# Attention scores of a transformer layer: whole float32 operands on four row groups of 32, in place of split parts over 128 rows

## The reference

```
q = (x @ Wq) -> 16 heads of 2*32;   k = (x @ Wk) -> 4 heads of 2*32;   v = (x @ Wv) -> 4 heads of 64
q1, q2 = rope(q[..., :32]), rope(q[..., 32:]);   k1, k2 likewise       # 4 heads of q share one of k and v
s1 = q1 @ k1.T / sqrt(32) + causal mask;   s2 = q2 @ k2.T / sqrt(32) + causal mask
out = (softmax(s1) - lam * softmax(s2)) @ v
out = group norm of out over time and channels, per head;   x = layernorm(x + out @ Wo)
x = layernorm(x + (silu(x @ up.T) * (x @ gate.T)) @ down.T)            # ternary up, gate, down
```

## Time and profile before

| what | us |
|---|---|
| median of 3 runs (lowest, highest) | 2625.27 (2624.8, 2626.22) |
| the profiled execution: its time, its span | 2625.6, 2623.8 |
| TensorE busy in the span | 2405.9 |
| VectorE busy | 1788.7 |
| ScalarE busy | 1412.5 |
| GpSimd busy | 814.8 |
| first and last start of a score matmul | 89.4, 2257.9 |

### The profile page before, as it was taken

How to read it: one execution, slowest core, us unless ns; L and a number is a source line. 1 busy time by engine, 2 the same in 40 slices (tenths; PEclk the granted TensorE clock), 3 DMA queues, 4 the chain that set the end, 5 groups by cost and what they waited for, 6 DMA issues and landing times.

```text
span 2623.8 us, 40656 instructions
## 1 busy us (share of the span) xinstructions
PE 2405.9 (92%) x14610; PEld 1424.2 (54%) x14610; DVE 1788.7 (68%) x3370; ACT 1412.5 (54%) x3462; POOL 814.8 (31%) x1344
## 2 busy tenths in 40 slices
PE   7689978789999999999999999999999989998999
PEld 4356554455655555555555556555555555543443
DVE  1467777878777777777777877787787777633343
ACT  1268755566655666666556666666656666420221
POOL 2323356644321333323221342323231222231122
PEclk9799988899999999999999999999999999999999
DMA  5756655555541212122622252313144311003000
GB/s 161 206 163 176 183 159 152 145 150 167 151 111 41 67 59 73 48 81 78 195 75 65 91 139 71 91 61 93 41 121 119 86 39 41 17 33 120 9 17 16
DMA packets 257591, 256.49 MB, mean 98 GB/s; under 512 B 31344, under 2 KB 199408, under 8 KB 255216
## 3 DMA queue, kind: packets, MB, share of 16 engines
q1 hardware_dynamic: 244864, 218.16, 29.5%
q10 hardware_dynamic: 12528, 35.73, 4.5%
HBM read 182.53 MB, written 71.30 MB: 97 GB/s over the span
## 4 chain that ended last, share of the span: by engine, by line
PE 70%; DVE 11%; ACT 6%; POOL 5%; issue 5%; DMA 1%; SPq 0%; ACTq 0%; POOLq 0%; DVEq 0%
PE F L703 17%; PE F L690 9%; PE PV L650 8%; PE F L712 8%; PE S L632 8%; PE F L673 7%; PE TB L617 7%; DVE nmax L953 4%; PE F L681 2%; ACT dt_long L757 2%; ACT e_short L766 2%; PE PV L653 2%; PE S L635 2%; POOL x_lo L937 2%; POOL hl L919 1%
## 5 line engine op out<-in xcount | busy, mean ns | idle before, releaser
L953 DVE TENSOR_REDUCE nmax<-S 128x1 f32<-128x1024 f32 (+7 forms) x1024 | 769.5, 752 | 434.1 <-PE S L635 429.7
L766 ACT ACTIVATE e_long<-S,nmax 128x768 f32<-128x768 f32 (+3 forms) x512 | 489.8, 957 | 301.4 <-DVE nmax L953 295.1
L632 PE MATMUL S<-kstk,qstk 128*128 128x384 f32 (+5 forms) x1536 | 552.3, 414 | 91.7 <-ACT e_long L766 71.2
L892 POOL TENSOR_SCALAR coef<-lsum,linv,neglam 128x1 f32<-128x1 f32 x512 | 176.0, 344 | 1223.0 <-DVE linv L1031 1222.3
L757 ACT ACTIVATE dt_long<-TB 128x512 f32<-128x512 f32 (+3 forms) x512 | 265.2, 518 | 425.1 <-PE TB L617 423.8
L632 PEld LDWEIGHTS S<-kstk,qstk 128*128 128x128 f32 x1536 | 268.2, 200 | 185.8 <-ACT e_long L766 65.3
L673 PE MATMUL F<-xT,wr 128*128 128x512 f32 x640 | 324.1, 637 | 4.4 <-DVE t L987 4.4
L1063 DVE SCALAR_TENSOR_TENSOR e_long<-e_long,coef 128x1024 f32<-128x1024 f32 (+3 forms) x256 | 287.6, 1123 | 37.6 <-POOL coef L892 37.4
L617 PE MATMUL TB<-ident,e_long 128*128 128x128 f32 x1664 | 272.9, 278 | 9.8 <-ACT dt_long L757 9.5
L766 ACT ACTIVATE e_short<-S,nmax 128x384 f32<-128x384 f32 (+3 forms) x512 | 269.2, 526 | 17.5 <-DVE nmax L953 17.1
L690 PE MATMUL F<-wo_sb,at_sb 128*128 128x512 f32 x512 | 243.0, 606 | 14.6 <-issue 11.0
(11 more groups left out here) (101 smaller groups left out, 3288.1 us busy)
## 6 DMA issues: line engine op xcount, KB each, us to landing
qstk<-dq SPq DMA_DIRECT2D x512, 128.0 KB, 3.2
dq<-hl SPq DMA_DIRECT2D x32, 1024.0 KB, 5.0
wr<-in_w_proj ACTq DMA_DIRECT2D x48, 512.0 KB, 3.7
kstk<-dk SPq DMA_DIRECT2D x64, 256.0 KB, 5.4
da<-ra SPq DMA_DIRECT2D x32, 512.0 KB, 2.7
at_sb<-da SPq DMA_DIRECT2D x32, 512.0 KB, 4.2
xs<-in_x ACTq DMA_DIRECT2D x36, 256.0 KB, 3.3
dk<-hl SPq DMA_DIRECT2D x8, 1024.0 KB, 4.9
```

The costliest lines, as they stand in the source:

```text
L632: nc.tensor.matmul(slot[:, h, :], qstk[:, duo % 4, 2 * r + m, :].bitcast(F32R), kstk[:, g % 2, m, h * w:(h + 1) * w].bitcast(F32R), start= ...
L766: nc.scalar.activation(e.rearrange("p (h w) -> p h w", h=parts), slot, ACT.Exp, bias=nmax[:, u % 8:u % 8 + 1], scale=1.0, accum_out=lsum[: ...
L953: nc.vector.tensor_reduce(nmax[:, u % 8:u % 8 + 1], bank_of(n, m), AX.XY, ALU.max, negate=True)\
```

## The change

q and k are no longer split. GpSimd writes the rotated values into `qk`, two DMAs store them, and the loads place the 32 rows of map 0 and the 32 rows of map 1 twice over the 128 partitions (rows 64h+32m). A head's scores are then float32 matmuls of 32 rows: row group 64h+32m computes map m of column half h into bank `S[m][:, h]`. A head with t = 0 has one half (two matmuls), any other two halves (four matmuls). Both maps of head n+1 are issued together at the end of step n, behind one wait: `s_exp >= 2n+2`, which is both exponents of head n. The matmuls in the middle of the step go. The two mask matmuls follow, and one semaphore increment tells of both maps.

The bit mask, the subtraction and the stage of the pipeline between them go, and with them one step of delay of the store. The planner's costs follow: only `score_cost(n + 1)` is charged to step n. The queues of ScalarE and, but for the bit mask, of VectorE keep their order.

```diff
 def score_cost(n):
     t = STEPS[n].t
-    return 0.0533 * (t + 1) + 0.1 * (1 + (t >= 4)) + 0.067
+    return 0.107 * (t + 1) / (2 if t else 1) + 0.35
...
-    c = 0.0
-    for k in (n, n + 1):
-        if 0 <= k < NH:
-            c += score_cost(k)
+    c = score_cost(n + 1) if 0 <= n + 1 < NH else 0.0
...
         def bank_of(n, m):
             t = STEPS[n].t
             w = (t + 1) * P
-            if t >= 4:
-                return S[m][:, :, 0:w // 2]
-            return S[m][:, n // 2 % 2:n // 2 % 2 + 1, 0:w]
+            return S[m][:, 0:halves(n), 0:w // halves(n)]
...
-                sp.wait_ge(s_lo, u + 1)
-                sp.dma_start(dst[:, :, :, job.h * BANK:(job.h + 1) * BANK].rearrange("a (e i) m t -> (i m) (a e) t", e=2),
-                             hl[:, :, :]).then_inc(s_hlst, 16)
+                sp.wait_ge(s_rot, u + 1)
+                for m in range(2):
+                    sp.dma_start(dst[m, :, :, job.h * BANK:(job.h + 1) * BANK].rearrange("(e i) h t -> (i h) e t", e=2),
+                                 qk[64 * m:64 * m + 64, u % 2, :, :]).then_inc(s_qkst[u % 2], 16)
...
-                for k in ended(st - 3, ("O",)):
+                for k in ended(st - 2, ("O",)):
                     store_rotated(k)
...
-            def scores(n, m):
-                b, c, t, r, duo = STEPS[n]
+            def scores(n):
+                t, r, duo = STEPS[n].t, STEPS[n].r, STEPS[n].duo
...
-                if SCORE_AFTER[2 * n + m]:
-                    pe.wait_ge(s_exp, SCORE_AFTER[2 * n + m])
-                slot = bank_of(n, m)
-                parts, w = slot.shape[1], slot.shape[2]
+                if n:
+                    pe.wait_ge(s_exp, 2 * n)
+                parts = halves(n)
+                w = (t + 1) * P // parts
                 for h in range(parts):
-                    nc.tensor.matmul(slot[:, h, :], qstk[:, duo % 4, 2 * r + m, :].bitcast(F32R),
-                                     kstk[:, g % 2, m, h * w:(h + 1) * w].bitcast(F32R),
-                                     start=True, stop=h < parts - 1)
-                nc.tensor.matmul(slot[:, parts - 1, w - P:w], ident_b[:, :], mask_b[:, :], start=False, stop=True)\
-                    .then_inc(s_score, 1)
+                    for m in range(2):
+                        rows = slice(64 * h + 32 * m, 64 * h + 32 * m + 32)
+                        nc.tensor.matmul(S[m][:, h, 0:w], qstk[rows, duo % 4, r, :], kstk[rows, g % 2, h * w:(h + 1) * w],
+                                         start=True, stop=h < parts - 1)
+                for m in range(2):
+                    last = nc.tensor.matmul(S[m][:, parts - 1, w - P:w], ident_b[:, :], mask_b[:, :], start=False, stop=True)
+                last.then_inc(s_score, 1)
...
-                if 0 <= n < NH:
-                    scores(n, 1)
...
                 if 0 <= n + 1 < NH:
-                    scores(n + 1, 0)
+                    scores(n + 1)
...
-                for k in ended(st - 2, ("O",)):
-                    u = ROT[k]
-                    dve.wait_ge(s_rot, u + 1)
-                    if u:
-                        dve.wait_ge(s_hlst, 16 * u)
-                    nc.vector.tensor_scalar(hl[:, 0:2, :].bitcast(I32), t4[:, 0:2, :].bitcast(I32), HI_BITS, None,
-                                            ALU.bitwise_and).then_inc(s_hi, 1)
```

More of the change, by code:

```diff
@@ L7 @@
 from concourse import mybir
-F32, F32R, F16, BF16 = mybir.dt.float32, mybir.dt.float32r, mybir.dt.float16, mybir.dt.bfloat16
-F8, I32 = mybir.dt.float8e4, mybir.dt.int32
+F32, F16, BF16 = mybir.dt.float32, mybir.dt.float16, mybir.dt.bfloat16
+F8 = mybir.dt.float8e4
 ACT = mybir.ActivationFunctionType
@@ L28 @@
 NEG = -3.0e38
-HI_BITS = -4096
 XS = 1024.0
@@ L65, with halves @@
         TURN[_n, _h] = len(TURN)
[L68 to L78, removed]
+def halves(n):
+    return 2 if STEPS[n].t else 1
 JOB = namedtuple("JOB", "kind b h i j")
@@ L287, in layer_kernel @@
              w_down.rearrange("(c p) n -> p c n", p=P)]
-    dq = nc.dram_tensor("dq", (B, 4, 2, DH, 8, T), F32, kind="Internal").ap()
-    dk = nc.dram_tensor("dk", (B, 2, DH, 8, T), F32, kind="Internal").ap()
+    dq = nc.dram_tensor("dq", (B, 4, 2, DH, 4, T), F32, kind="Internal").ap()
+    dk = nc.dram_tensor("dk", (B, 2, DH, KV, T), F32, kind="Internal").ap()
     dv = nc.dram_tensor("dv", (B, NT, P, 256), F32, kind="Internal").ap()
@@ L321, in layer_kernel @@
         t4 = sb("t4", [P, 4, BANK])
-        hl = sb("hl", [P, 4, BANK])
+        qk = sb("qk", [P, 2, 2, BANK])
         vst = sb("vst", [P, 2, 256])
-        qstk = sb("qstk", [P, 4, 4, P])
-        kstk = sb("kstk", [P, 2, 2, T])
+        qstk = sb("qstk", [P, 4, 2, P])
+        kstk = sb("kstk", [P, 2, T])
         vkv = sb("vkv", [P, 2, NT, 64])
@@ L389, in layer_kernel @@
         s_gn = sem("s_gn")
-        s_hlst = sem("s_hlst")
+        s_qkst = [sem(f"s_qkst{k}") for k in range(2)]
         s_vst = sem("s_vst")
@@ L412, in layer_kernel @@
         s_rot = sem("s_rot")
-        s_hi = sem("s_hi")
-        s_lo = sem("s_lo")
         s_xhi = sem("s_xhi")
@@ L446, in freed, with stored @@
             eng.wait_ge(s_ffree[k % 2], k // 2 + 1)
+        def stored(eng, u):
+            eng.wait_ge(s_qkst[u % 2], 32 * (u // 2 + 1))
         def bank_of(n, m):
@@ L492, in load_q @@
                 b, c, t, _, _ = STEPS[n]
-                sp.wait_ge(s_hlst, 16 * (ROT_OF[b, t // 4, 2 + c // 2] + 1))
+                stored(sp, ROT_OF[b, t // 4, 2 + c // 2])
                 if duo >= 4:
-                    sp.wait_ge(s_score, 2 * heads_of(duo - 4)[1] + 2)
-                at = 4 * (c % 2)
-                src = dq[b, c // 2, :, :, at:at + 4, t * P:(t + 1) * P].rearrange("a d m t -> (a d) m t")
+                    sp.wait_ge(s_score, heads_of(duo - 4)[1] + 1)
+                at = 2 * (c % 2)
+                src = dq[b, c // 2, :, :, at:at + 2, t * P:(t + 1) * P].rearrange("m d h t -> (m d) h t")
                 for half in range(2):
@@ L502, in load_k @@
                 b, kv = divmod(g, KV)
-                sp.wait_ge(s_hlst, 16 * (ROT_OF[b, 1, 0] + 1))
+                stored(sp, ROT_OF[b, 1, 0])
                 if g >= 2:
[L505 to L508, removed]
+                    sp.wait_ge(s_score, 32 * (g - 1))
+                src = dk[b, :, :, kv, :].rearrange("m d t -> (m d) t")
+                for half in range(2):
+                    sp.dma_start(kstk[64 * half:64 * half + 64, g % 2, :], src).then_inc(s_kin[g % 2], 16)
             def load_v(g):
@@ L618, in turn @@
                 last.then_inc(s_tb, 1)
-            def scores(n, m):
-                b, c, t, r, duo = STEPS[n]
+            def scores(n):
+                t, r, duo = STEPS[n].t, STEPS[n].r, STEPS[n].duo
                 g = n // 32
-                if r == 0 and m == 0:
+                if r == 0:
                     pe.wait_ge(s_qin[duo % 4], 32 * (duo // 4 + 1))
-                if n % 32 == 0 and m == 0:
-                    pe.wait_ge(s_kin[g % 2], 64 * (g // 2 + 1))
-                if SCORE_AFTER[2 * n + m]:
-                    pe.wait_ge(s_exp, SCORE_AFTER[2 * n + m])
-                slot = bank_of(n, m)
-                parts, w = slot.shape[1], slot.shape[2]
-                for h in range(parts):
-                    nc.tensor.matmul(slot[:, h, :], qstk[:, duo % 4, 2 * r + m, :].bitcast(F32R),
-                                     kstk[:, g % 2, m, h * w:(h + 1) * w].bitcast(F32R),
-                                     start=True, stop=h < parts - 1)
-                nc.tensor.matmul(slot[:, parts - 1, w - P:w], ident_b[:, :], mask_b[:, :], start=False, stop=True)\
-                    .then_inc(s_score, 1)
+                if n % 32 == 0:
+                    pe.wait_ge(s_kin[g % 2], 32 * (g // 2 + 1))
+                if n:
+                    pe.wait_ge(s_exp, 2 * n)
+                parts = halves(n)
+                w = (t + 1) * P // parts
+                for h in range(parts):
+                    for m in range(2):
[5 more added lines that the diff above has]
+                last.then_inc(s_score, 1)
             def values(duo):
@@ L913, in _ @@
                 for k in ended(st - 1, ("O",)):
+                    u = ROT[k]
                     freed(pool, k)
-                    nc.gpsimd.tensor_tensor(t4[:, 0, :], t4[:, 0, :], t4[:, 2, :], ALU.subtract)
-                    nc.gpsimd.tensor_tensor(t4[:, 1, :], t4[:, 1, :], t4[:, 3, :], ALU.add).then_inc(s_rot, 1)
-                for k in ended(st - 2, ("O",)):
-                    pool.wait_ge(s_hi, ROT[k] + 1)
-                    nc.gpsimd.tensor_tensor(hl[:, 2:4, :], t4[:, 0:2, :], hl[:, 0:2, :], ALU.subtract).then_inc(s_lo, 1)
+                    if u >= 2:
+                        stored(pool, u - 2)
+                    nc.gpsimd.tensor_tensor(qk[:, u % 2, 0, :], t4[:, 0, :], t4[:, 2, :], ALU.subtract)
+                    nc.gpsimd.tensor_tensor(qk[:, u % 2, 1, :], t4[:, 1, :], t4[:, 3, :], ALU.add).then_inc(s_rot, 1)
```

(9 more changed lines are left out.)

## The result

The changed kernel took 3189.03 us (median of four runs, 3188.04 to 3192.9) against 2625.74 us for the kernel before on the same chip: a ratio of 1.2148 (95% interval 1.2127 to 1.2169), so 563 us slower. The forecast was 3040 us with a range of 2860 to 3200. The profiled execution has a span of 3187.0 us.

The account below looks back on a forecast made before the run. TensorE was taken as the bound. Work 2018, new waits 610 and lower clock 50 gave 2678 us of attention; with start 89 and tail 275, 3042, stated as 3040 us, range 2860 to 3200.

Parts of the forecast that it names:

- The score work costs the same: TensorE's score matmuls: four row groups together give back what four slots a column take; 437 us against 438 before.
- The rival of one pass: Score packs cost one pass in place of two, as the planner's price says: 126 us less, 2915 us; chance 0.12.
- that of groups in pairs: Row groups of the score packs run only in pairs, or passes in turn: 253 us more, 3290 or more; chance 0.1.
- that of a poorer overlap: The four row groups overlap less well than two column groups did: about 75 us more, 3115 us; chance 0.15.
- The wait in odd steps: At the end of steps with a short head, scores wait for ScalarE's second exponent, behind an eviction: 320 us.
- The wait in even steps: At the end of steps with a long head, scores wait for VectorE's chain and the second exponent: 290 us.
- The new waits don't shrink because others run ahead: Denies the rival that ScalarE and VectorE run ahead, so new waits are half as long: 2840 us; chance 0.13.
- the 0.37 at which that case began: Faster case, 2500 us, chance 0.04: decides where the new wait is under 0.37 us a step; forecast had 1.2.
- the remainder: What the attention stretch loses beyond TensorE's work and new waits, taken as lower clock: 50 us, ends 0 and 241.
- the old 241 us: Waits, gaps and lower clock in the 2172 us in which scores ran in the kernel before.
- 2018 (work at full clock): TensorE's work in the attention stretch: fill 961, scores 437, turns 277, values 343 us.
- The plan: New planner prices move fill from tail to attention, +88 and -88 us: still TensorE's work, so no gain.

Follow-up runs that it names:

- e9: e1 with one wait more: VectorE's maximum of map 0 waits for the scores of both maps; 3188 us.
- e7: The changed kernel with the planner's old prices, so fill stands where it stood before; 3206 us.
- e3: The changed kernel with ScalarE's exponent of map 1 put ahead of the eviction of the second half of head n-3; 2942 us.
- e4: The changed kernel with VectorE, in even steps, taking the maximum of map 1 directly behind that of map 0; 3152 us.
- e1: The kernel before, old score matmuls and plan, with both maps of head n+1 at the end of step n behind both exponents of head n; 3041 us.
- e8: e1 with the planner's new prices; 3050 us.
- e2: The changed kernel with packs cut in two, one per map, placed and waited for as in the kernel before; 2933 us.

## Why the forecast held, and what it mis-sized

**The score work costs the same: right.** 437 us were forecast. The packs' slots, first start to the next kind of work, have medians of 1.20, 1.09, 0.98 and 0.88 us for t = 7 to 4 and 0.55 to 0.77 for t = 0 to 3; 64 of each are 427 us. (Four instructions in 1.77 us are 0.44 each and not 0.43, as the forecast has it; over its 3.95 us of passes this is some 3%, 8 us in all.) The rival of one pass (2915 us), that of groups in pairs (3290) and that of a poorer overlap (3115) are out; e9 shows the same from the other side: its old matmuls, measured in the same way, take 416 us, and exchanging them for packs at the same plan and with the same two waits (e7) costs 17 us.

**The wait in odd steps: right.** 320 us forecast, 329 measured from start to start; e3 shows that ScalarE's eviction is what stands in it: with the exponent ahead of it 112 us are left.

**The wait in even steps: right in place, 48 us too long.** 290 us forecast, 242 measured. e4 shows that VectorE's chain sets it. The forecast let the chain begin behind the last mask without saying what it would be if it didn't; that start alone, as e9 against e1 shows, is worth 148 us at the old plan.

**The new waits don't shrink because others run ahead.** That rival had 2840 us; 571 us of waits against 610 forecast put it out. Nor was the kernel faster: the new wait is 1.1 us a step, far from the 0.37 at which that case began.

**What the sum mis-sized is the remainder.** The forecast kept 50 of the old 241 us for clock and all else. Measured: 2838 - 2018 (work at full clock) - 571 (new waits) = 249 us. With the waits 39 us shorter than forecast, 199 - 39 = 160 us more in this stretch; start and tail took 15 less. That is the whole difference, 3187 against 3042; a step takes 5.5 us in this stretch where 5.1 were forecast. The forecast gave this term ends of 0 and 241 us, and 249 lies outside them.

Two things went into it. The first is the clock: at 0.93 about 400 us of the stretch ran at 1.2 GHz, against 130 before, and each costs at most half of itself, so at most 200 us in all and 135 more than before. The forecast carried the clock of before into a kernel that it had just filled with idle gaps. The second it put at nothing: gaps of TensorE ahead of other work than the scores. With each slot taken at the clock of its moment, those of over 0.25 us add up to 124 us in this stretch, against 140 in the stretch of before. Those ahead of transposes did shrink, from 88 to 33 us, as the forecast had it; those ahead of fill grew. By difference the clock would then be some 125 of the 249 us, an estimate; no run changed the clock alone.

**Luck.** The measured time lies 11 us inside the upper end of the range. Had the waits been as long as forecast, with this remainder, it would have been some 39 us more and outside. The short waits of the even steps hid part of the mis-sized remainder.

**The plan: right that moved work gains nothing.** The tail fell by 98 us, and e7 and e8 put the plan's net worth at -17 and +9 us.

## What to carry to other kernels

When an instruction gathers two results that were made apart, ask first what the consumers did with the time between them: here the maximum of map 0 and the reuse of its banks ran in it, and losing that cost nearly all of the 563 us, though the matmuls cost about the same. A queue's order that is harmless with a step of slack becomes the critical path when the slack goes, so the order of each engine behind a new wait has to be read again. And where a change adds waits on TensorE, the clock of the profile before need not be the clock of the profile after.

## What the runs showed of the hardware

How many rows the matmuls use did not set the granted clock: it was 0.984 with twice the packs of 32 rows and few waits (e2), and with the same waits and plan 0.943 with packs (e7) and 0.944 with matmuls over 128 rows (e9). Float32 matmuls on four row groups interleave by themselves: the first instructions of all four start within 0.02 us, then the second ones together, 0.45 us later for 448 columns, though the program has them matmul by matmul.
